# Per-node sums of a graph network: tile sums stored in DRAM and gathered again, or added in place into one turned tile in SBUF

## The chip, the cores and the metric

The kernel runs on one core of one Trainium2 chip. The time is the device time of one launch in microseconds; a kernel's time is the median of its runs. One more execution was recorded by the profiler; all rows below are of that one.

## What is computed

A graph of 12,500 nodes and 412,500 edges, sorted by their destination node, goes through two small networks. What matters here are the five places in which rows of edges are added up by destination.

```python
x = _layernorm(x + _L0_gnn_ref(x, edges, edge_weight, ...))    # two GCN convolutions: in each
    msg = xw[r] * norm[:, None]                                # one row of 16 (after moving W) for an edge
    out = segment_sum(msg, c, num_segments=num_nodes)
x = _layernorm(x + _L1_gnn_ref(x, edge_attr_8, src, dst, ...))
    n, e = _ln(_mlp(node_feat)), _ln(_mlp(edge_feat))          # encoders, width 64
    for s in range(2):
        ce = concatenate([e, n[senders], n[receivers]])
        e = e + _ln(_mlp(ce, ...)) * g + beta                  # 64 features for an edge
        agg = segment_sum(e, receivers, num_segments=num_nodes)
        n = n + _ln(_mlp(concatenate([n, agg]), ...))
    return _mlp(n)
```

## The kernel before

**Tiles and steps.** The edges are padded to 3232 tiles of 128; since they are sorted, a tile's destinations lie in a window of 128 nodes that begins at its first destination. One step of an edge loop takes G = 8 tiles; there are 403 steps (`NIST`). Nodes stand as 128 partitions times C = 98 (12544 places).

**The program** is a row of blocks with a barrier between them: tables, weights, edge loop g1, `conv1`, edge loop g2, `conv2`, node phase ne, edge loop s0, node phase n0, edge loop s1, node phase n1. g1 carries the first convolution's messages (16 columns) and the edge encoder (64): FS = 80 columns; g2 carries the second convolution's messages (16); s0 and s1 are the two edge blocks (64 columns, `expand`).

**One step.** `drive` (L573 is its loop of 8 steps an iteration, 50 iterations, with the steps before and behind written out) calls each engine's `step`; the engines meet by semaphores alone, and each runs its own instructions in order. A chunk of 8 tiles goes through stages a step apart (`L_BW` to `L_SUM`). POOL issues 8 indirect gathers of 128 rows for the senders (L720) into one of 8 buffers, and waits for the buffer: for the message product's mark `v_msg` in g1 and g2, for PE's mark `p_pre` in s0 and s1. SP loads their indices (L689) every fourth step, and in s0 and s1 the copies of destination numbers (L700) and four of the eight windows `Bw` of receivers' rows (L669); ACT loads the other four and `z` (L680). DVE makes the one-hot `P` (edge against place in the window, L608), in s0 and s1 the turned one-hot `Pt` for the receivers (L741), in g1 and g2 the message columns of `R` (L749), then the layer norm (L754, L756, Newton steps L140 to L149, `R` at L762) and in s0 the sum `rT` (L734). ACT does the squares, the activation `hT`, and copies.

**The sums.** PE multiplies for each of the 8 tiles P by R (L863: P as 128x128 weights, FS columns moving) into the PSUM tile `psw`: row w of a tile's product is the sum for the w-th node of its window. ACT copies psw to `sg` (L793), which frees psw (`a_seg`), and stores it (L808) to the tensor `seg_d` in DRAM. A node may have edges in several tiles, whose windows overlap only where one tile ends and the next begins. So behind each loop (`Sums`) POOL gathers each tile's last row (26 gathers, L931), PE turns them (L954), DVE multiplies and scans along the chain of tiles (L971, L974), PE turns the result back (L960), it is added to `seg_d` by DMA, and POOL gathers each node's row (98 gathers, L944) into `agg`. After g1 conv1 takes 16 of the 80 columns and POOL adds the other 64, with the norm's gain, to the second half of `NA`, which holds [nodes | sums] 128 wide; n0 and n1 add their sums to the same half, plus count times bias, and turn its 128 columns as the MLP's input in groups of four columns of nodes (8 stages).

## Time and profile before

| | us |
|---|---|
| median of 3 runs | 23702.86 (23700.19 to 23767.57) |
| the profiled execution | 23779.25 |
| its span, first to last instruction | 23777.4 |
| mean granted TensorE clock | 0.627 of 2.4 GHz |

| engine | busy us | share | instructions |
|---|---|---|---|
| TensorE (PE), matmul | 12398.6 | 52% | 61970 |
| VectorE (DVE) | 7767.6 | 33% | 22504 |
| ScalarE (ACT) | 2986.5 | 13% | 5247 |
| GpSimd (POOL) | 12971.1 | 55% | 13518 |

Shares over the span mix eleven blocks with different limits; the table of stretches below, with one row for a block, is to be read before them. "Idle before" in a row is time in which the engine stood still just before that instruction, and the name behind it is what ended that; "remote" is a semaphore of another engine that the profile can't place, "issue" is no wait that it shows.

### The profile page before, as it was taken

How to read it: one execution, taken by the hardware profiler on the slowest of the kernel's cores; microseconds unless marked ns; L12 is line 12 of the kernel's file. 1: busy time of each engine (PE TensorE's matmuls, PEld its weight loads, DVE VectorE, ACT ScalarE, POOL GpSimd, SP SyncE). 2: the span in 40 equal slices, each digit the busy share in tenths (PEclk: the TensorE clock that was granted, in tenths of full speed). 3: DMA queues.
4: the chain of work that ended last, by engine and by line, in shares of the span. 5: the costliest groups of instructions: out<-in, count | busy, mean ns of one | idle time of the engine just before them, and what ended most of it. 6: DMA issues, size and time to landing. Idle time of an engine off the chain costs nothing. (4 is left out here: it accounts for less than half of the span.)

```text
span 23777.4 us, 256036 instructions
## 1 busy us (share of the span) xinstructions
PE 12398.6 (52%) x61970; PEld 9600.5 (40%) x61970; DVE 7767.6 (33%) x22504; ACT 2986.5 (13%) x5247; POOL 12971.1 (55%) x13518
## 2 busy tenths in 40 slices
PE   0555565554232322325555656655556666666665
PEld 0444444443222222223444444444434444544454
DVE  2333333333111111112334434333333344343342
ACT  0222222221000000001111111111111111111111
POOL 2556565655666666662555555455435555555552
PEclk9566555565555555555667666666666666666675
DMA  1122222221000000001333333333323333333330
GB/s 50 52 54 56 54 55 55 55 55 47 12 11 11 11 11 11 11 11 22 99 102 107 107 102 104 103 105 104 103 60 94 100 98 99 99 99 98 99 101 14
DMA packets 2031268, 1570.78 MB, mean 66 GB/s; under 512 B 1340117, under 2 KB 1497177, under 8 KB 2029449
## 3 DMA queue, kind: packets, MB, share of 16 engines
q10 hardware_dynamic: 932082, 898.84, 11.7%
q0 software_dynamic: 446304, 295.04, 8.6%
q1 hardware_dynamic: 652511, 373.44, 5.7%
q14 instruction: 319, 2.61, 0.0%
q8 instruction: 52, 0.85, 0.0%
HBM read 961.50 MB, written 604.22 MB: 66 GB/s over the span
## 5 line engine op out<-in xcount | busy, mean ns | idle before, releaser
L720 POOL DMA_INDIRECT s_gt<-ta_d,s_ix x6448 | 6187.6, 960 | 5660.7 <-DMA s_ix<-in_src_s 2441.5
L863 PE MATMUL psw<-g_R,g_P 128*128 128x80 f32 (+1 forms) x12896 | 2673.2, 372 | 4261.8 <-ACT g_sg L793 3414.1
L863 PEld LDWEIGHTS psw<-g_R,g_P 128*128 128x128 f32 x12896 | 2568.8, 305 | 4795.9 <-issue 3827.8
L720 POOL DMA_INDIRECT g_gt<-xs_d,g_ix x3224 | 3048.8, 946 | 2077.7 <-DVE g_R L749 1106.8
L720 POOL DMA_INDIRECT g_gt<-ys_d,g_ix x3224 | 3049.7, 946 | 1798.9 <-issue 990.0
L608 DVE TENSOR_TENSOR g_P<-ps,dlT 128x1024 f32<-128x1024 f32 x806 | 985.3, 1222 | 5610.4 <-remote 4927.6
L863 PEld LDWEIGHTS psw<-s_R,s_P 128*128 128x128 f32 x12896 | 1908.9, 222 | 1705.1 <-issue 1702.8
L863 PE MATMUL psw<-s_R,s_P 128*128 128x64 f32 x12896 | 1877.4, 298 | 1057.3 <-issue 1020.0
L831 PE MATMUL ps<-e_w,s_hT 128*128 128x128 f32 x6448 | 1342.6, 375 | 1956.5 <-ACT s_hT L788 1679.1
L848 PE MATMUL ps<-s_Pt,s_Bw 128*64 128x128 f32 x12896 | 1535.7, 370 | 1009.8 <-issue 1008.2
L831 PEld LDWEIGHTS ps<-e_w,s_hT 128*128 128x128 f32 x6448 | 1181.8, 274 | 2084.2 <-ACT s_hT L788 1346.1
L848 PEld LDWEIGHTS ps<-s_Pt,s_Bw 128*64 128x64 f32 x12896 | 1118.1, 189 | 1358.4 <-issue 1356.4
L831 PE MATMUL ps<-e_w,g_hT 128*128 128x128 f32 x3224 | 768.4, 416 | 1266.4 <-issue 795.4
L734 DVE SCALAR_TENSOR_TENSOR s_rT<-ps,gct,s_z 128x512 f32<-128x512 f32 x403 | 302.1, 750 | 3179.4 <-DMA e_d<-s_rT 3081.6
L851 PE MATMUL ps<-s_z,zw 128*128 128x512 f32 x1612 | 1280.0, 881 | 84.3 <-issue 83.7
L831 PEld LDWEIGHTS ps<-e_w,g_hT 128*128 128x128 f32 x3224 | 700.7, 320 | 1325.3 <-issue 830.7
L793 ACT ACTIVATE g_sg<-psw 128x640 f32<-128x640 f32 (+1 forms) x806 | 395.7, 491 | 6599.3 <-remote 5304.3
L608 DVE TENSOR_TENSOR s_P<-psw,dlT 128x1024 f32<-128x1024 f32 x806 | 980.3, 1216 | 611.6 <-remote 529.4
L788 ACT ACTIVATE s_hT<-ps 128x512 f32<-128x512 f32 x806 | 480.4, 596 | 4303.1 <-remote 3728.9
L754 DVE TENSOR_REDUCE s_ss<-s_sq 128x8 f32<-128x512 f32 x806 | 547.1, 679 | 1371.9 <-issue 795.6
L741 DVE TENSOR_SCALAR s_Pt<-s_dl,iop 128x1024 f32<-128x1024 bf16 x806 | 612.8, 761 | 991.0 <-remote 806.1
L779 ACT ACTIVATE s_sq<-ps 128x512 f32<-128x512 f32 x806 | 481.4, 597 | 3553.5 <-issue 2016.2
(289 smaller groups left out, 12961.8 us busy)
## 6 DMA issues: line engine op xcount, KB each, us to landing
s_dl<-dl_d SPq DMA_DIRECT2D x404, 512.0 KB
seg_d<-s_sg ACTq DMA_DIRECT2D x806, 256.0 KB
seg_d<-g_sg ACTq DMA_DIRECT2D x403, 320.0 KB
z_d<-g_rT ACTq DMA_DIRECT2D x403, 256.0 KB
s_z<-z_d ACTq DMA_DIRECT2D x403, 256.0 KB, 3.0
s_Bw<-tb_d ACTq DMA_DIRECT2D x3224, 32.0 KB
s_Bw<-tb_d SPq DMA_DIRECT2D x3224, 32.0 KB
s_gt<-ta_d,s_ix POOLq DMA_INDIRECT x6448
```

What stands on the lines that cost most here:

```text
L608: return eng.tensor_tensor(P[:, :, :], bc(columns.rearrange("p (o e) -> p o e", o=1), [128, G, 128]), bc(dlT[:, bass.ds(j * G, G)].rearran ...
L720: eng.indirect_dma_start(out=gt[k][:, s, :], out_offset=None, in_=table[:, :], in_offset=bass.IndirectOffsetOnAxis(ap=ix[h][:, r * G + s:r ...
L734: eng.scalar_tensor_tensor(out=rT[k][:, :], in0=ps[5][:, :], scalar=gct[1][:, 0:1], in1=zt[kz][:, :], op0=ALU.mult, op1=ALU.add).then_inc( ...
L741: eng.tensor_scalar(Pt[t % 2][:, :], dl[h][:, t % 2 * G * 128:(t % 2 + 1) * G * 128], iop[:, 0:1], None, ALU.is_equal).then_inc(v_pt.sem, 1)
L754: eng.reduce_sum(ss[:, :], sq[k][:, :, :], axis=AX.X)
L779: eng.activation(sq[k][:, :, :].rearrange("p s f -> p (s f)"), ps[2 + k][:, :], ACT.Square).then_inc(a_sq.sem, 1)
L788: eng.activation(hT[k][:, :], ps[k][:, :], ACT.Silu).then_inc(a_h.sem, 1)
L793: eng.activation(sg[k][:, :].rearrange("p (t f) -> p t f", t=G), psw[:, 0:G * SP_].rearrange("p (t f) -> p t f", t=G)[:, :, 0:FS], ACT.Cop ...
L831: eng.matmul(ps[2 + k][:, 128 * q:128 * q + 128], hT[k][:, 128 * q:128 * q + 128], mlp[0][:, :], start=q == 0, stop=False, skip_group_chec ...
L848: eng.matmul(ps[k][half:half + 64, 128 * q:128 * q + 128], Bw[(b - L_PRE) % 4][:, t, :], Pt[k][:, 128 * t:128 * t + 128], start=False, sto ...
L851: eng.matmul(ps[k][:, :], (e_w0 if attr else zw)[:, :], zt[(b - L_PRE) % DZ][:, :], start=not expand, stop=True, skip_group_check=True).th ...
L863: last = eng.matmul(psw[:, SP_ * t:SP_ * t + FS], P[k][:, s, :], R[k][:, s, :], start=True, stop=True)
```

## The change

One SBUF tile `acc` of 128 partitions by 12544 + 128 columns holds the sums turned: column = node, row = feature. Rows 0 to 63 are the edge features, 64 to 79 the convolution's messages, row 80 the number of edges of a node. It is zeroed on POOL (at the end of the weights' block; rows 64 to 79 again in conv1) and kept over all loops.

PE's tile product is turned: R is the weights (80, 16 or 64 columns), P moves (128 columns), and the result is feature by place in the window, in `psw[LO:HI, 128 t]`. The 8 products come in two halves, each with its own mark `p_seg`. At the start of a step (stage `L_ACC` = 7) DVE loads four addresses for a half, waits for that half of the chunk before, and adds four times 128 columns of psw to `acc` at a column known only at run time, with a drain behind each since windows overlap; `v_acc` frees the half of psw. The norm's gain is the scalar of that addition (`accg`); g2 has none. Its bias, times the node's count in row 80, comes into the node MLP as a row of the weights `nb_wa`.

Gone are seg_d, sg, ACT's copy and store of it, the class `Sums` with its gathers, scans, transposes and stores, and the tables for them. conv1 and conv2 take their 16 rows from `acc` by 98 small matmuls (`by_node`) and add them from PSUM. The nodes' tile is 64 wide (`ND`); the node phases turn 64 columns and multiply `acc` directly by `nb_wa` (four matmuls a group); their POOL programs go.

`Pt` moves from DVE to ACT: `off` = Square(dl - p), then Relu(1 - off), two passes of 128x1024 behind `hT`; SP's load of dl and PE wait for its mark `a_pt`.

```diff
+        L_BW, L_Z, L_PT, L_PRE, L_LN, L_SEG, L_ACC, L_SUM, L_ST = 2, 2, 3, 4, 5, 6, 7, 7, 7
...
+        def half_done(eng, sem, j, off, h):
+
+            v = (j - off) * 2 + h + 1
+            if not isinstance(v, int) or v > 0:
+                eng.wait_ge(sem.sem, v + sem.base)
...
+            LO = 0 if mlp else 64
+            HI = LO + FS
...
-                            done(eng, v_pt, j, 3)
+                            done(eng, a_pt, j, 3)
...
+                        if stage(j, L_ACC):
+                            for h in range(2):
+                                _, at = nc.values_load_multi_w_load_instructions(
+                                    basei[32:33, bass.ds((j - L_ACC) * G + 4 * h, 4)], engines=[mybir.EngineType.DVE], min_val=0, max_val=N,
+                                    skip_runtime_bounds_check_because="a tile's first dst is a node's number")
+                                half_done(eng, p_seg, j, L_ACC, h)
+                                for t in range(4):
+                                    sums = acc[LO:HI, bass.ds(at[t], 128)]
+                                    new = psw[LO:HI, 512 * h + 128 * t:512 * h + 128 * t + 128]
+                                    if scale is None:
+                                        last = eng.tensor_tensor(sums, new, sums, ALU.add)
+                                    else:
+                                        last = eng.scalar_tensor_tensor(out=sums, in0=new, scalar=scale[LO:HI, 0:1], in1=sums,
+                                                                        op0=ALU.mult, op1=ALU.add)
+                                    if t < 3:
+                                        eng.drain()
+                                last.then_inc(v_acc.sem, 1)
+                                eng.drain()
...
-                        if stage(j, L_PT) and expand:
-                            t = b - L_PT
-                            h = (t // 2) % 2
-                            done(eng, p_pre, j, L_PT + 2)
-                            eng.wait_ge(s_dl[h].sem, (i * 2 + t // 4 + 1) * 16 + s_dl[h].base)
-                            eng.tensor_scalar(Pt[t % 2][:, :], dl[h][:, t % 2 * G * 128:(t % 2 + 1) * G * 128], iop[:, 0:1], None,
-                                              ALU.is_equal).then_inc(v_pt.sem, 1)
...
-                            done(eng, p_seg, j, L_LN + 2)
+                            half_done(eng, p_seg, j, L_LN + 2, 1)
...
-                        if stage(j, L_SEG):
+                        if stage(j, L_SEG) and attr:
                             k = (b - L_SEG) % 2
-                            done(eng, p_seg, j, L_SEG)
-                            landed(eng, s_so, 1, i, b, L_SEG + 2)
-                            eng.activation(sg[k][:, :].rearrange("p (t f) -> p t f", t=G),
-                                           psw[:, 0:G * SP_].rearrange("p (t f) -> p t f", t=G)[:, :, 0:FS],
-                                           ACT.Copy).then_inc(a_seg.sem, 1)
-                            if attr:
-                                done(eng, p_rt, j, L_SEG)
-                                landed(eng, s_ro, 1, i, b, L_SEG + 2)
-                                eng.activation(rT[k][:, :], ps[5][:, :], ACT.Copy, scale=gct[0][:, 0:1]).then_inc(a_rt.sem, 1)
+                            done(eng, p_rt, j, L_SEG)
+                            landed(eng, s_ro, 1, i, b, L_SEG + 2)
+                            eng.activation(rT[k][:, :], ps[5][:, :], ACT.Copy, scale=gct[0][:, 0:1]).then_inc(a_rt.sem, 1)
+                        if stage(j, L_PT) and expand:
+                            t = b - L_PT
+                            h = (t // 2) % 2
+                            done(eng, p_pre, j, L_PT + 2)
+                            eng.wait_ge(s_dl[h].sem, (i * 2 + t // 4 + 1) * 16 + s_dl[h].base)
+                            done(eng, a_pt, j, L_PT + 1)
+                            eng.activation(off[:, :], dl[h][:, t % 2 * G * 128:(t % 2 + 1) * G * 128], ACT.Square,
+                                           bias=niop[:, 0:1]).then_inc(a_off.sem, 1)
+                            done(eng, a_off, j, L_PT)
+                            eng.activation(Pt[t % 2][:, :], off[:, :], ACT.Relu, scale=-1.0, bias=one1[:, 0:1]).then_inc(a_pt.sem, 1)
...
-                        if stage(j, L_ST):
-                            k = (b - L_ST) % 2
-                            done(eng, a_seg, j, L_ST)
-                            settle(eng, s_m[0])
-                            eng.dma_start(seg_rows[:, bass.ds((j - L_ST) * (G * FS), G * FS)], sg[k][:, :]).then_inc(s_so[k].sem, 16)
...
-                            done(eng, a_seg, j, L_SEG + 1)
-                            for s in range(G):
-                                t = SLOT_TILE[s]
-                                last = eng.matmul(psw[:, SP_ * t:SP_ * t + FS], P[k][:, s, :], R[k][:, s, :],
-                                                  start=True, stop=True)
-                            last.then_inc(p_seg.sem, 1)
+                            for h in range(2):
+                                half_done(eng, v_acc, j, L_SEG + 1, h)
+                                for t in range(4 * h, 4 * h + 4):
+                                    s = TILE_SLOT[t]
+                                    last = eng.matmul(psw[LO:HI, 128 * t:128 * t + 128], R[k][:, s, :], P[k][:, s, :],
+                                                      start=True, stop=True)
+                                last.then_inc(p_seg.sem, 1)
...
-        class Sums:
...
+        def by_node(eng, sem):
+
+            for n, (q, m) in enumerate(BANKS):
+                for k in range(m):
+                    last = eng.matmul(ps[n][:, 16 * k:16 * k + 16], accn[64:80, q + k, :], ident[64:80, 64:80], start=True, stop=True)
+                last.then_inc(sem.sem, 1)
...
-                sums_of("ns80", seg80_d, 80, agg, lambda eng: eng.tensor_tensor(NA[:, :, 64:128], cb, bb, ALU.mult))
...
-                    eng.tensor_tensor(agg[:, :, 0:64], agg[:, :, 0:64], gb, ALU.mult).then_inc(g_agg.sem, 1)
-                    eng.wait_ge(*g_agg(1))
-                    eng.tensor_tensor(NA[:, :, 64:128], NA[:, :, 64:128], agg[:, :, 0:64], ALU.add)
+                    eng.wait_ge(*p_agg(len(BANKS)))
+                    eng.memset(acc[64:80, :], 0.0)
...
+                    by_node(eng, p_agg)
...
-                    eng.tensor_tensor(tx[:, :, :], tx[:, :, :], agg[:, :, 64:80], ALU.add)
+                    for n, (q, m) in enumerate(BANKS):
+                        eng.wait_ge(*p_agg(n + 1))
+                        eng.tensor_tensor(tx[:, q:q + m, :], tx[:, q:q + m, :], bank(n), ALU.add)
...
-                sums_of("ns16", seg16_d, 16, agg)
...
-                            eng.matmul(ps[1][0:64, 0:W], w0[:, :], xT[k][:, 0:W], start=True, stop=True).then_inc(n_h.sem, 1)
+                            last = eng.matmul(ps[1][0:64, 0:W], w0[:, :], xT[k][:, 0:W], start=True, stop=wa is None, skip_group_check=True)
+                            for i in range(m if wa is not None else 0):
+                                last = eng.matmul(ps[1][0:64, 128 * i:128 * i + 128], wa[:, :], accn[0:81, g + i, :],
+                                                  start=False, stop=i == m - 1, skip_group_check=True)
+                            last.then_inc(n_h.sem, 1)
```

How the instructions of DVE stand in the loop of g2, each step ending with the message product `g_R`. Before (`g_gt` are the gathered rows, `ew` the weights, `dlT` the destinations):

```order
L608 ISA [waits e_pseg]
L608 TENSOR_TENSOR g_P<-ps,dlT 128x1024
L749 REGISTER_ALU [waits e_g5]
L749 TENSOR_TENSOR g_R<-g_gt,ew 128x128
L573 REGISTER_ALU
```

And after, one half of the adds and what follows the second:

```order
L740 TENSOR_TENSOR g_R<-g_gt,ew 128x128
L712 ISA
L712 TENSOR_LOAD basei
L599 ISA
L720 ISA [waits e_pseg]
L720 TENSOR_TENSOR acc<-psw,acc 16x128
L720 ISA
...
L580 ISA [waits e_pseg]
L580 TENSOR_TENSOR g_P<-ps,dlT 128x1024
L571 ISA
L740 REGISTER_ALU [waits e_g6]
```

Before, P was the first thing behind the wait for PE's tile sums; now eight adds and two address loads stand between g_R and the next P.

DVE in the loop of s0, from the norm's `s_R` to the one-hot. Before:

```order
L762 TENSOR_TENSOR s_R<-ps,s_yy 128x512 [waits e_prt]
L599 ISA [waits e_prt]
L734 SCALAR_TENSOR_TENSOR s_rT<-ps,gct,s_z 128x512 [waits e_ro0]
L591 REGISTER_ALU
L741 TENSOR_SCALAR s_Pt<-s_dl,iop 128x1024 [waits e_dl1,e_ppre]
L591 REGISTER_ALU
L608 ISA [waits e_pseg]
L608 TENSOR_TENSOR s_P<-psw,dlT 128x1024
```

After:

```order
L753 TENSOR_TENSOR s_R<-ps,s_yy 128x512 [waits e_prt]
L712 ISA
L712 TENSOR_LOAD basei
L599 ISA
L722 ISA [waits e_pseg]
L722 SCALAR_TENSOR_TENSOR acc<-psw,accg,acc 64x128
L722 ISA
...
L571 ISA [waits e_prt]
L732 SCALAR_TENSOR_TENSOR s_rT<-ps,gct,s_z 128x512 [waits e_ro0]
L580 ISA [waits e_pseg]
L580 TENSOR_TENSOR s_P<-ps,dlT 128x1024
```

The adds stand ahead of s_rT and its wait; s_Pt has left the engine.

## Rows read from the trace of the kernel before

**Rows 1.** The table of stretches, one for a block: us, busy (instructions), clock, DMA
```profile
521.50:5653.00 5131.50, 2986.84 (x12493) 2313.26 (x12493) 1955.94 (x6449) 1265.07 (x2016) 3048.77 (x3224) 0.60 0.21 54
...
5956.00:10792.00 4836.00, 1438.09 (x6448) 1405.04 (x6448) 573.63 (x807) 112.13 (x404) 3049.67 (x3224) 0.50 0.10 11
...
11021.50:11267.00 245.50, 240.49 (x902) 153.06 (x902) 91.19 (x400) 70.27 (x126) 0.00 (x0) 0.58 0.12 27
11267.00:17382.00 6115.00, 3588.39 (x20553) 2644.74 (x20553) 2418.94 (x6852) 693.37 (x1211) 3095.39 (x3224) 0.69 0.38 104
17382.00:17763.50 381.50, 186.53 (x1006) 132.19 (x1006) 149.11 (x531) 70.43 (x127) 148.69 (x128) 0.70 0.18 35
17763.50:23193.00 5429.50, 3516.04 (x18941) 2638.15 (x18941) 2149.78 (x6449) 691.86 (x1211) 3092.19 (x3224) 0.68 0.37 98
23193.00:23777.40 584.40, 349.08 (x1227) 242.41 (x1227) 167.19 (x573) 72.52 (x126) 148.98 (x128) 0.55 0.07 13
```

The busy columns are PE, PEld, DVE, ACT, POOL.

**Rows 2.** POOL's waits in g1, g2 and s1: us in total, times, longest
```profile
POOL g_gt L720 <- DVE g_R L749: 1106.8, 243, 15.1
...
POOL g_gt L720 <- DVE g_R L749: 749.0, 97, 15.7
...
POOL s_gt L720 <- DMA s_ix<-in_src_s: 857.3, 97, 171.8
```

**Rows 3.** Timeline of g1: start, us, engine, line, operation, [idle before]
```profile
3020.91 1.23 DVE L608 TENSOR_TENSOR g_P<-ps,dlT 128x1024 f32<-128x1024 f32 x1 [4.15 <-remote]
...
3022.06 3.70 PE L863 MATMUL psw<-g_R,g_P 128*128 128x80 f32 x16
...
3023.12 0.95 POOL L720 DMA_INDIRECT g_gt<-xs_d,g_ix  x1 [5.61 <-DVE g_R L749]
```

**Rows 4.** Timeline of g2
```profile
8024.00 1.22 DVE L608 TENSOR_TENSOR g_P<-ps,dlT 128x1024 f32<-128x1024 f32 x1 [26.71 <-remote]
...
8026.20 0.95 POOL L720 DMA_INDIRECT g_gt<-ys_d,g_ix  x1 [7.88 <-DVE g_R L749]
...
8028.05 1.22 DVE L608 TENSOR_TENSOR g_P<-ps,dlT 128x1024 f32<-128x1024 f32 x1 [2.63 <-PE psw L863]
```

**Rows 5.** Between the loops: a group of gathers, then timeline rows of n0, conv1, conv2
```profile
L944 POOL DMA_INDIRECT n_agg<-seg_d,gidx x196 | 186.1, 949 | 73.3 <-issue 59.2 <-DMA seg_d<-n_ns_L 14.1
...
17472.18 1.08 POOL L944 DMA_INDIRECT n_agg<-seg_d,gidx  x1 [7.09 <-DMA seg_d<-n_ns_L]
...
5870.97 15.04 DVE L1089 TENSOR_TENSOR tx<-xf,dis 128x1568 f32<-128x1568 f32 x1 [145.04 <-PEq L32]
...
11000.51 1.79 DVE L1136 TENSOR_TENSOR agg<-agg,ys 128x1568 f32<-128x1568 f32 x1 [140.67 <-PEq L32]
```

**Rows 6.** DVE's groups by line and form: busy us, mean ns, idle before
```profile
L741 DVE TENSOR_SCALAR s_Pt<-s_dl,iop 128x1024 f32<-128x1024 bf16 x806 | 612.8, 761 | 991.0 <-remote 806.1 <-issue 176.6 <-DMA s_dl<-dl_d 8.3
...
L145 DVE TENSOR_TENSOR s_tt<-s_yy 128x8 f32<-128x8 f32 x2418 | 415.5, 172 | 180.2 <-issue 1.2
...
L1315 DVE TENSOR_TENSOR n_rr<-ps,n_yy 128x256 f32<-128x256 f32 x48 | 20.4, 425 | 3.9 <-issue 0.4
...
L968 DVE COPY ns_LT<-ps 80x128 f32<-80x128 f32 x26 | 6.4, 287 | 36.5 <-PE ps L954 35.1
```

**Rows 7.** Line 665 in s1, duration in ns: smallest, median, largest
```profile
L665 ACTq TENSOR_LOAD <-basei x329: 311/315/338, 18608.5 to 22997.1; - x165
```

**Rows 8.** DVE's waits in s0, 12000 to 17000 us
```profile
DVE s_rT L734 <- DMA e_d<-s_rT: 2612.7, 276, 29.9
```

**Rows 9.** PE's groups in s0 and s1, from the page: busy us, mean ns
```profile
L863 PE MATMUL psw<-s_R,s_P 128*128 128x64 f32 x12896 | 1877.4, 298 | 1057.3 <-issue 1020.0
...
L848 PE MATMUL ps<-s_Pt,s_Bw 128*64 128x128 f32 x12896 | 1535.7, 370 | 1009.8 <-issue 1008.2
```

**Rows 10.** Line 573, DVE at the loop's end in s1: ns, first and last start
```profile
L573 DVEq COMPARE_BRANCH  x41: 62/63/63, 18686.3 to 22965.0; - x41
...
L573 DVEq FUSED_REGOPS  x41: 62/63/63, 18690.3 to 22968.5; - x41
```

361 lines of the change are left out of this document (112 added, 249 removed).

## The prediction

> **What bounds the kernel now.** I read the table of stretches first, then who waits for whom on POOL, then two cycles of the timeline, then the durations. By the stretches [rows 1] four edge loops of 403 steps take 21,512 of the 23,777 us: 12.73, 12.00, 15.17 and 13.47 us a step for g1, g2, s0 and s1; what lies between and behind them takes 303.0 us for conv1 (from g1's end to g2's start), 229.5 for conv2, 245.5 for ne, 381.5 for n0 and 584.4 for n1. In every loop POOL's busy time is 3,049 to 3,095 us: 8 gathers a step at 0.95 us, 1.25 us from start to start. So 10.0 us a step is POOL issuing, and 2.0 to 5.2 us is POOL stopped. VectorE (DVE) is busy 4.9, 1.4, 6.0 and 5.3 us a step: never the bound now.
>
> Why does POOL stop? In g1 and g2 it waits for DVE's `g_R` (L749), 1,107 and 749 us, in 243 and 97 waits; in s1 the long waits are for the index load, 857 us [rows 2]. The timeline shows what is behind the first two. In g1 [rows 3] POOL had stopped at 3017.51 (3023.12 less 5.61); DVE starts the one-hot P only at 3020.91, after 4.15 us idle, the product g_R follows it, and POOL starts 2.2 us behind P's start: 3.4 + 2.2 = 5.6 us. Two steps go into each such cycle: 20 + 5.6 us. In g2 [rows 4] DVE had been idle for 26.71 us, P starts at 8024.00, and POOL's stop was 7.88 us; the next step then follows 4.05 us behind (8028.05). Four steps go into such a cycle: 40 + 7.9 us = 12.0 each, which is the loop's mean. PE's signals that DVE waits for come late while POOL issues without a break, and soon after it stops. I take that as a given of the trace; its cause I can't see.
>
> **The change, part by part.** The sum is made against the profiled execution: 23,779 us, 76 us (0.3%) above the median of 23,703; the forecast is brought to the median at the end. 0.3%, some 71 us, is what a measurement can tell.
>
> *Gone, and sure.* Between the loops the sums' machinery vanishes. In n0 the 90 us of last rows, transposes, scan and stores ahead of the first gather of node sums (17382 to 17472.18) go, and the first node group no longer waits for 24 gathers, each 1.32 us ((186.1 + 73.3)/196), 32 us [rows 5]; the rest of its 291 us behind the first gather is about the pace of the groups themselves, for which ne needs 245.5 us [rows 1]. The four new matmuls of a group cost some 12 us in all: -110. n1 likewise, -122. conv1: 217 us of sums (5653 to 5870) go, and a DVE operation that takes 15.04 us beside POOL's long additions takes 1.79 at conv2 without them [rows 5]; there are two such, -27 together. In come 98 matmuls at up to 0.37 us (the means of [rows 9]), 36 us, and the adds of four banks, about 8: +44. Sum: -200. conv2: 208 us of sums (10792 to 11000.5 [rows 5]) against +45: -163. In the tables three stores and a scan go: -15, from nearly nothing to 30. **Between the loops: -610 us**, between -500 and -680.
>
> A rule of the Trainium skill fits these rows (SBUF — State Buffer, "Who interferes with whom"): a DVE operation with two SBUF inputs and a GpSimd one exclude each other for a whole instruction. The trace agrees at conv1 with 15.04 against 1.79 us. By the same rule the new adds, which read one operand from PSUM, would not be held by POOL; the sum takes nothing for it.
>
> *Added on DVE, every step:* eight adds of 128 elements a partition from PSUM into `acc`, a drain behind each, and two loads of four addresses. An add lies between the copy of 128 from PSUM, 0.287 us, and the 256-element operation from PSUM, 0.425 [rows 6]; the middle is 0.345, with 0.07 for the drain (what lies between DVE's small operations that drain, 180.2 us in 2418 [rows 6]) and 0.065 for the address's register work, my guess between nothing and the 0.13 that would double it: 0.48, eight times 3.85. An address load is 0.31 us on ScalarE (ACT) [rows 7]; with its registers 0.4, twice 0.8. In all **4.65 us a step** (4.2 in g2, whose adds have no scalar), bounds 3.6 and 5.6. DVE loses the receivers' one-hot in s0 and s1, 0.76 us [rows 6]; ACT gets two passes of 128x1024 for it (each at most about DVE's 1.22 for as many elements [rows 4]) and loses the tile sums' copy and store; it is busy 11 to 25% now and I count nothing. DVE's step becomes 10.4, 5.8, 10.8 and 10.1 us with its gaps: as long as POOL's 10.0, where it was half.
>
> *Where the adds lie.* They stand ahead of P and g_R, behind the same late signal. In **g1**, first half's signal now comes when PE is halfway through its 16 matmuls (3.7 us [rows 3], so 1.85 early); the second half's adds and loads, and the rest of the first, come on top: 4.65 - 1.85 = 2.8 us longer for POOL's stop, in a cycle of two steps +1.4 a step. Some of the 243 waits are shorter than that cycle's, so I take +1.15: **+463 us**, bounds 0 (adds done before the signal matters) and +2.3 a step, +937. In **g2** 4.2 - 1.8 = 2.4 us in four steps, +0.6: **+242**; bounds 0 and, if a cycle holds only three steps because a step in the quick part now takes 5.8 instead of 4.05 us, (30 + 9.7)/3 = 13.2, +490. In **s0** POOL doesn't wait for DVE, and DVE itself waits before L734 for 2,613 us in 330 steps (5,000 us at 15.17), 7.9 each [rows 8]: the adds stand right ahead of that wait and fill it: **0**, bounds -0.43 and +0.6 a step. The lower bound is PE's: tile sums cost 1877.4/12896 = 0.146 us each now, and the matmul with the shape they get (64 columns of weights, 128 moving), L848, 0.119 [rows 9]; 16 of them are 0.43 us a step, which I count at nothing, since POOL and not PE stands at 15.17. The stores gone are 256 KB a step of DMA traffic; nothing waited for them. In **s1** PE's products wait for R, which comes 4 us later in a step with 3 us of room: +0.15, **+60**, bounds -0.43 and +0.6.
>
> Loops: 463 + 242 + 0 + 60 = **+765 us**. With -610: **+155**; 23,779 + 155 = 23,934 for the profiled execution, 23,858 against the median: **23,860 us**, 0.7% slower.
>
> **The rivals.** *The adds cost nothing* (faster). DVE idles 26.7 us before the late signal in g2 and 4 to 8 in g1; if half signals come early enough for the adds to run in that idle time, the loops stay as they are and only the 610 us count: 23,093; with PE's 0.43 us in both s loops (-345) 22,750. For it: DVE is 28 to 40% busy, and POOL's 10 us are untouched. Against it: in [rows 3, 4] P and g_R start the moment the signal comes, so anything put between moves POOL's start.
>
> *The adds in full* (slower). The half signal comes no earlier, because both halves are late together; g1 +937 and g2 at three steps a cycle +490; 1,427 - 610 = +817, 24,520 against the median. This decides once the four loops lose more than 610/1612 = 0.38 us a step on average; the forecast has 0.47.
>
> *DVE's program gets too long.* In s1 DVE passes its loop's end in 4.0 us (18686.3 to 18690.3) [rows 10] where the branch takes 0.06; such a pass in each of 50 iterations of g1 and s0 as well is up to 400 us: on top of the forecast 24,260. For it: the bodies grow from 155 and 173 rows to 332, drains not counted. Against it: DVE has room in s0, and POOL runs on meanwhile.
>
> **Chances.** The forecast 0.42, adds hidden 0.25, in full 0.20, long program 0.13. The forecast's own terms spread by some 200 us either way, so it lends 0.09 to faster and 0.12 to the same. Faster by over 0.3%: 0.34; within: 0.12; slower: 0.54. The forecast's own range is 23,650 to 24,100; to leave out no more than 2 in 10 the range goes from 23,050, the hidden adds, to 24,600, the adds in full.
>
> **What would show it.** In the profile after: g1 near 13.9 and g2 near 12.6 us a step, s0 near 15.2, s1 near 13.6; conv1 near 100 us, conv2 near 65, n0 near 270, n1 near 460. POOL's stop in g2 near 10 us every fourth step, with eight adds between DVE's late start and g_R; one add at 0.35 us, start to start 0.48. In s0 the wait of L734 shrunk by about 4 us a step. It is wrong if g1 or g2 keeps its step, if POOL comes to wait for DVE every step, or if s0 and s1 move by more than 0.6 us a step either way: then PE's signals, not POOL, set those loops.

## The result: 4.9% slower, and the profile after

The changed kernel takes 24,885 us (median of 4 runs, 24,864 to 24,901); the kernel before, run beside it, 23,724 (23,700 to 23,768). The ratio is 1.0487, with a 95% interval of 1.0467 to 1.0506. The forecast was 23,860 us with a range up to 24,600: slower was right, the size was not, and the time lies outside the range.

The profiled execution spans 24,890 us, 1,113 more than before's 23,777. The table of stretches of the changed kernel, cut as in [rows 1]: after the stretch come its us, then the busy time (instructions) of PE, PE's weight loads, DVE, ACT and POOL, the granted clock, the DMA share and GB/s.

```profile
521.00:6471.00 5950.00, 3139.02 (x12482) 2477.58 (x12483) 3063.01 (x9665) 963.45 (x1612) 3050.56 (x3224) 0.58 0.10 25
6471.00:6581.50 110.50, 99.48 (x358) 81.87 (x358) 21.27 (x64) 10.07 (x27) 10.65 (x1) 0.50 0.04 14
6581.50:11592.00 5010.50, 1478.58 (x6451) 813.20 (x6451) 1508.85 (x4031) 0.00 (x0) 3049.60 (x3224) 0.52 0.06 6
11592.00:11895.50 303.50, 279.28 (x1097) 194.75 (x1096) 111.05 (x425) 70.28 (x126) 0.00 (x0) 0.58 0.10 22
11895.50:18077.00 6181.50, 3694.96 (x20533) 2582.71 (x20533) 3225.64 (x9645) 1357.17 (x1613) 3049.35 (x3224) 0.71 0.31 86
18077.00:18381.50 304.50, 289.55 (x1118) 199.87 (x1118) 110.88 (x453) 70.40 (x126) 0.00 (x0) 0.61 0.10 24
18381.50:24465.00 6083.50, 3430.21 (x18941) 2367.42 (x18941) 2965.73 (x9270) 1358.67 (x1613) 3049.11 (x3224) 0.70 0.27 70
24465.00:24890.30 425.30, 377.21 (x1319) 258.12 (x1319) 117.70 (x469) 72.53 (x126) 0.00 (x0) 0.56 0.01 2
```

In order they are g1, conv1, g2, conv2 with ne, s0, n0, s1, n1. Against [rows 1] the blocks between the loops give what was promised: conv1 303.0 to 110.5, conv2 with ne 475.0 to 303.5, n0 381.5 to 304.5, n1 584.4 to 425.3; together -600 us (-610 forecast). The four loops lose 1,713 us (765 forecast): g1 12.73 to 14.76 us a step, g2 12.00 to 12.43, s0 15.17 to 15.34, s1 13.47 to 15.09. So two terms of the forecast are wrong: **g1, +2.03 a step for +1.15, and s1, +1.62 for +0.15**.

**g1.** POOL's waits in g1 of the changed kernel (us in total, times, longest); the first row answers to 1,107 us in 243 waits in [rows 2]:

```profile
POOL g_gt L700 <- DVE g_R L740: 1813.9, 286, 18.3
POOL g_gt L700 <- issue: 1001.5, 2937, 10.6
POOL g_gt L700 <- DMA g_ix<-in_src_s: 47.3, 1, 47.3
```

POOL still waits for DVE, longer. What does DVE wait for? First g1 of before, the three largest rows:

```profile
DVE g_P L608 <- remote: 1386.7, 198, 36.9
DVE g_ss L754 <- issue: 1108.0, 191, 34.2
DVE g_ss L754 <- ACT g_sq L779: 246.7, 203, 4.9
```

and g1 of the changed kernel:

```profile
DVE acc L722 <- issue: 1571.0, 2953, 6.0
DVE g_mq L142 <- issue: 180.7, 269, 1.5
DVE g_P L580 <- issue: 153.5, 392, 1.8
DVE g_yy L144 <- issue: 136.4, 211, 1.3
DVE g_tt L140 <- issue: 132.2, 202, 1.3
DVE acc L722 <- remote: 77.3, 12, 22.9
```

Before, DVE stood still twice in every second step: some 200 times for P, 7 us each, and some 200 times for `g_ss`, 6 us each (the profile calls these "issue", so the word alone is no proof that an engine waited for nothing). Now the waits put down to other engines and to DMA come to some 170 us in the whole loop, and DVE's idle time lies in thousands of short gaps ("issue": nothing that the profile shows released it). A step of DVE holds 7.60 us busy (3063.01/403) and 7.16 idle. Its largest group in g1, the adds (busy, mean ns, then idle before them):

```profile
L722 DVE SCALAR_TENSOR_TENSOR acc<-psw,accg,acc 80x128 f32 x3216 | 1116.6, 347 | 1723.3 <-issue 1571.0 <-remote 77.3 <-PE psw L853 69.9
```

From start to start an add takes (1116.6 + 1723.3)/3216 = 0.88 us, loads and waits included, where the forecast had 0.48, or 0.58 with the address loads (4.65/8). The timeline of g1 (start, us, engine, line, [idle before]) shows both kinds:

```profile
3019.29 0.35 DVE L722 SCALAR_TENSOR_TENSOR acc<-psw,accg,acc 80x128 f32 x1 [2.88 <-issue]
3021.42 0.35 DVE L722 SCALAR_TENSOR_TENSOR acc<-psw,accg,acc 80x128 f32 x1 [1.79 <-issue]
3022.85 0.35 DVE L722 SCALAR_TENSOR_TENSOR acc<-psw,accg,acc 80x128 f32 x1 [1.08 <-issue]
3023.35 0.35 DVE L722 SCALAR_TENSOR_TENSOR acc<-psw,accg,acc 80x128 f32 x1 [0.15 <-issue]
3023.76 2.00 PE L853 MATMUL psw<-g_P,g_R 128*80 128x128 f32 x8 [8.73 <-DVE acc L722]
3024.44 0.35 DVE L722 SCALAR_TENSOR_TENSOR acc<-psw,accg,acc 80x128 f32 x1 [0.73 <-issue]
3024.94 0.35 DVE L722 SCALAR_TENSOR_TENSOR acc<-psw,accg,acc 80x128 f32 x1 [0.15 <-issue]
```

An undisturbed add stands 0.50 us behind the last; but three of the first half's four came 1 to 3 us late, beside POOL's last gathers and right behind them, and PE waited 8.73 us for them, because the adds free `psw`.

The stops of POOL, counted in both traces as gaps between two gathers, show what became of the forecast's cycle. Before, POOL stopped 195 times for over 5 us, 5.6 on average. After, it stops 180 times for over 5 us, 9.1 on average (the forecast: 5.6 + 2.8 = 8.4), and 191 more times for 1 to 5 us, 1.5 on average, where before it did so twice. The longer stops are 1.4 us of the lost 2.0 a step, the new short ones 0.7. In g2 the waits for g_R read

```profile
POOL g_gt L700 <- DVE g_R L740: 928.7, 191, 16.5
```

against 749.0 in [rows 2]. The stops over 5 us didn't grow (7.7 us before, 7.5 after), they came more often: 118 for 97.

**s1.** POOL's waits in s1, after; its long ones are still for the index load and for released buffers:

```profile
POOL s_gt L700 <- DMA s_ix<-in_src_s: 1656.8, 92, 396.6
POOL s_gt L700 <- issue: 941.4, 2978, 3.9
POOL s_gt L700 <- remote: 435.9, 118, 12.2
POOL s_gt L700 <- PE ps L840: 299.5, 36, 14.4
```

and before, beside the 857.3 for the index load in [rows 2]:

```profile
POOL s_gt L720 <- remote: 629.9, 196, 12.0
POOL s_gt L720 <- PE ps L851: 21.8, 5, 8.7
```

One wait of each index row lies ahead of the loop's first gather, while the nodes are computed: 171.8 us before, 396.6 after, when POOL has no work there any more. Without it the index load is waited for 575 us longer (1260.2 for 685.5), PE's products, which release POOL's buffers, 278 us longer, and "remote" 194 us shorter: together 659 us, the lost 1.6 us a step. SP issues the index load, behind the load of `dl` in one queue, and that waits for `Pt`, which ACT now makes; PE's products wait for `Pt` too.

### The profile page after: what moved, and what is told of

Read it like the earlier page. It is cut to its first block and busy times, and to the rows that moved or that the text cites. A ratio compares the mean times of both kernels' runs of the same rounds, so it can differ in the third digit from the quotient of the medians.

```text
span 24890.3 us, 296537 instructions
## 1 busy us (share of the span) xinstructions
PE 12793.7 (51%) x62338; PEld 8979.1 (36%) x62338; DVE 11285.5 (45%) x34276; ACT 3904.1 (16%) x5246; POOL 12323.2 (50%) x13007
## 3 DMA queue, kind: packets, MB, share of 16 engines
q14 instruction: 1189, 9.74, 0.1%
## 5 line engine op out<-in xcount | busy, mean ns | idle before, releaser
L853 PE MATMUL psw<-g_P,g_R 128*80 128x128 f32 (+1 forms) x12896 | 3069.8, 418 | 6303.0 <-DVE acc L720 2421.8
L722 DVE SCALAR_TENSOR_TENSOR acc<-psw,accg,acc 64x128 f32 (+1 forms) x9672 | 3333.1, 345 | 5298.9 <-issue 4569.5
L853 PEld LDWEIGHTS psw<-g_P,g_R 128*80 128x80 f32 (+1 forms) x12896 | 2104.2, 192 | 7533.4 <-DVE acc L720 2651.0
L853 PE MATMUL psw<-s_P,s_R 128*64 128x128 f32 x12896 | 2245.9, 330 | 2550.7 <-DVE acc L722 1383.7
L853 PEld LDWEIGHTS psw<-s_P,s_R 128*64 128x64 f32 x12896 | 1776.9, 167 | 3558.1 <-DVE acc L722 1793.0
L720 DVE TENSOR_TENSOR acc<-psw,acc 16x128 f32 x3224 | 933.8, 290 | 3242.3 <-issue 2265.2
L580 DVE TENSOR_TENSOR s_P<-ps,dlT 128x1024 f32<-128x1024 f32 x806 | 984.1, 1221 | 225.3 <-issue 221.0
L784 ACT ACTIVATE g_rT<-ps,gct 128x512 f32<-128x512 f32 x403 | 277.0, 687 | 4302.9 <-remote 3036.2
L794 ACT ACTIVATE s_Pt<-s_off,one 128x1024 f32<-128x1024 bf16 x806 | 925.6, 1148 | 26.4
L791 ACT ACTIVATE s_off<-s_dl,niop 128x1024 bf16<-128x1024 bf16 x806 | 918.6, 1140 | 10.6 <-DMA s_dl<-dl_d 10.6
```

The lines of the kernel that those rows point to most:

```text
L580: return eng.tensor_tensor(P[:, :, :], bc(columns.rearrange("p (o e) -> p o e", o=1), [128, G, 128]), bc(dlT[:, bass.ds(j * G, G)].rearran ...
L720: last = eng.tensor_tensor(sums, new, sums, ALU.add)
L722: last = eng.scalar_tensor_tensor(out=sums, in0=new, scalar=scale[LO:HI, 0:1], in1=sums, op0=ALU.mult, op1=ALU.add)
L791: eng.activation(off[:, :], dl[h][:, t % 2 * G * 128:(t % 2 + 1) * G * 128], ACT.Square, bias=niop[:, 0:1]).then_inc(a_off.sem, 1)
L794: eng.activation(Pt[t % 2][:, :], off[:, :], ACT.Relu, scale=-1.0, bias=one1[:, 0:1]).then_inc(a_pt.sem, 1)
L853: last = eng.matmul(psw[LO:HI, 128 * t:128 * t + 128], R[k][:, s, :], P[k][:, s, :], start=True, stop=True)
```

## Experiments

The hypotheses, by letters that the texts on record use too: **R**, the address loads and register instructions of the adds are slow while POOL issues; **N**, the number and time of DVE's instructions (its step is as long as POOL's, so all of it counts, wherever it stands); **W**, the place of the adds between the late signal and g_R; **P**, `Pt` by two ACT operations, 2.3 us in place of DVE's 0.76; **F**, DVE's program fetched anew in every iteration.

The runs were made on five chips, each with the kernel before beside them. The chips differ: the kernel before took 23,509 us on chip A1 and 23,739 on A3, near the 23,724 of the result, but 18,410, 18,419 and 18,413 on B2, B4 and B5. Each chip was used once, so whether the chip makes the difference or its state at that time isn't shown. On B the loops of *ptact* and *best* run at POOL's own 10.0 us a step, or up to 0.2 above. Only ratios within a chip count. The table gives them with their intervals, and us a step from POOL's 89th gather of a loop to its last (the first steps left out, so most values are some 0.1 under those of the stretches). The row "before" is of the profile shown ahead; A1's own is 0.9% faster by its median, some 0.1 us a step, so that a difference of 0.1 there means nothing.

```
kernel           chip  ratio to before          g1     g2     s0     s1
before           A     1                        12.62  11.94  15.07  13.36
changed          A     1.0487 (1.0467-1.0506)   14.64  12.38  15.21  14.95
fixed            A1    1.0317 (1.0298-1.0336)   13.60  12.18  15.20  14.66
noadd            A1    1.0010 (1.0001-1.0020)   12.50  11.72  15.27  14.51
pad              A1    1.0400 (1.0381-1.0420)   13.06  12.10  15.20  14.34
merged           A1    1.0172 (1.0153-1.0191)   13.34  11.79  15.24  14.54
after_again      A3    1.0470 (1.0433-1.0507)   14.57  12.33  15.21  14.95
pt_back          A3    1.0256 (1.0220-1.0291)   14.43  12.36  14.60  14.34
pt_act_again     A3    1.0406 (1.0366-1.0445)   12.63  11.95  15.44  15.23
best_again       A3    0.9517 (0.9485-0.9549)   12.53  11.76  13.92  13.36
ptact            B2    1.0009 (0.9999-1.0018)   10.02  10.03  10.16   9.99
busy             B2    1.0858 (1.0840-1.0876)   11.03  10.92  11.11  11.31
late             B2    1.0472 (1.0455-1.0490)   10.63  10.02  11.95  10.48
best             B2    0.9763 (0.9747-0.9780)   10.02  10.01  10.15  10.17
late_again       B4    1.0466 (1.0447-1.0486)   10.64  10.02  11.91  10.51
late_pt          B4    1.0492 (1.0472-1.0513)   10.62  10.02  11.57  10.94
best_pause       B4    1.2860 (1.2839-1.2882)   13.45  13.45  13.64  13.91
late_third       B5    1.0457 (1.0438-1.0475)   10.62  10.03  11.86  10.49
after_third      B5    1.0421 (1.0404-1.0438)   10.81  10.02  11.33  10.73
best_pause1      B5    1.1739 (1.1719-1.1758)   12.24  12.14  12.25  12.79
```

### Chip A1: the adds taken apart

*fixed*: the eight adds go to fixed columns, so the address loads and register work are gone (the sums land in the wrong places).

```diff
-                                _, at = nc.values_load_multi_w_load_instructions(
-                                    basei[32:33, bass.ds((j - L_ACC) * G + 4 * h, 4)], engines=[mybir.EngineType.DVE], min_val=0, max_val=N,
...
-                                    sums = acc[LO:HI, bass.ds(at[t], 128)]
+                                    sums = acc[LO:HI, 128 * t:128 * t + 128]
```

> The changed kernel, but each add goes to a fixed column of acc (0, 128, 256 or 384) instead of the tile's own: no address load and no address register work on VectorE; the eight adds, their drains and waits stay. (The node sums are therefore not placed.) In the changed kernel g1 takes 14.76, g2 12.43, s0 15.34 and s1 15.09 us a step, and in each loop some 2,000 register instructions of VectorE last over 0.6 us, 1,550 to 1,780 us in all, about 4 us a step. Theory R (register work and address loads are what is slow while GpSimd issues): they are gone, g1 falls to about 12.8 to 13.2, s1 to about 13.6; in all about 23,400. Theory F (VectorE's long loop body is fetched anew in each iteration and starved): the body still has some 390 instructions in g1 and s0, other instructions take over the slow starts, g1 stays above 14, in all 24,400 or more. Theory W (the adds' own 3.8 us behind the late signal): g1 near 14.3, in all about 24,500.

g1 gets back 1.04 of its 2.02 us a step, g2 0.20, s1 0.29. So about half of g1's loss is the address work (R), less than R had forecast (g1 at 12.8 to 13.2). Of the 2,000 long ones that the text above counts in g1, some 770 are register instructions and address loads; the rest are drains. The adds in g1 of *fixed*, and what DVE waits for there:

```profile
L719 DVE SCALAR_TENSOR_TENSOR acc<-psw,accg,acc 80x128 f32<-80x128 f32 x3148 | 1088.7, 346 | 986.7 <-issue 403.2 <-remote 365.3 <-PE psw L850 62.9
```

```profile
DVE g_ss L742 <- ACT g_sq L767: 912.5, 87, 31.8
```

The "issue" gaps ahead of the adds fall from 1,571 to 403 us, and DVE waits for others again. The add itself (346 ns) costs the same.

*noadd*: no adds at all; the waits stay, and `psw` is freed at once (the sums are left out).

> The changed kernel without the adds: VectorE waits for each half of the tile sums and frees it at once, nothing is added (the node sums are left out). All theories expect what lies between the loops to stay as in the changed kernel, some 600 us less than before. If the adds are the whole loss, g1 returns to 12.7, g2 to 12.0, s1 to 13.5 and s0 to 15.2 us a step or less: about 23,100 in all. If moving the receivers' one-hot to ScalarE is what costs s1, s1 stays near 15.1: about 23,700.

g1 and g2 are 0.12 and 0.22 us a step under before: all that these two loops lose hangs on the adds and their address work. But s1 stands at 14.51, 1.15 above before, **without an add in the kernel**: most of s1's loss has another cause. POOL's waits in s1 of *noadd*:

```profile
POOL s_gt L700 <- DMA s_ix<-in_src_s: 1209.2, 61, 386.6
POOL s_gt L700 <- PE ps L826: 548.8, 43, 14.3
```

Without its first wait the index load stands at 823 us, 137 above before; PE's products stand 527 above.

*pad*: the kernel before with 28 drains at the end of DVE's step, as many more instructions as the change adds.

```diff
+                        for _ in range(28):
+                            eng.drain()
```

> The kernel before with 28 drains more at the end of VectorE's step: its loop bodies grow from about 259, 44, 283 and 265 recorded instructions to about 480, 270, 500 and 490, as long as in the changed kernel, with about 1 to 2 us of engine time a step, no register work, no address load and no wait. Theory F: the instruction packets of its queue rise from about 10 in a loop (253 in s1) to about 250 to 300 in each; VectorE starts late while GpSimd issues, and g1 and s1 rise by 0.5 to 1.5 us a step: 24,100 to 24,900. Theories R and W: nothing is behind the signal and VectorE has 5 us of room, so within 0.3% of 23,724.

4% from drains alone: g1 +0.44, g2 +0.16, s0 +0.13, s1 +0.98. DVE had no free room in s1, although its busy share there was 5.3 of 13.5 us [rows 1]. In g1 the drains, which stand behind g_R, cost a fifth of what the adds do. F had forecast this size (24,100 to 24,900; it came to 24,470), R and W nothing; a price on the number of DVE's instructions (N) gives it as well.

*merged*: one add a step. PE adds up the eight tiles in one bank over a window that begins at the step's first destination (1024 sorted edges touch far fewer than 128 nodes here, which this version relies on).

```diff
-                                for t in range(4):
-                                    sums = acc[LO:HI, bass.ds(at[t], 128)]
...
+                            sums = acc[LO:HI, bass.ds(at[0], 128)]
...
+                            for s in range(G):
+                                last = eng.matmul(psw[LO:HI, o:o + 128], R[k][:, s, :], P[k][:, s, :],
+                                                  start=s == 0, stop=s == G - 1)
```

> The changed kernel with one add a step instead of eight: TensorE sums the eight tiles of a step into one window in PSUM that begins at the step's first destination (the 1024 edges of a step span at most 34 nodes in these inputs, which the kernel relies on), in one of two banks; VectorE adds those 128 columns to acc: one address load, one add. Its loop body shrinks to about 300 instructions. All theories expect the loss in the loops to go: g1 12.7 to 13.0, g2 12.0, s0 15.0 and s1 13.5 or less, 23,100 in all. Theory F with a threshold between 283 and 300 instructions would leave a part in g1 and s0.

g1 +0.72, g2 -0.15, s1 +1.18, which is *noadd*'s. At 1.7% above before it missed what all had forecast (23,100). As to F, the queue of the instructions (packets, MB, share) in the changed kernel's page:

```profile
q14 instruction: 1189, 9.74, 0.1%
```

Before has 319 packets, *fixed* 799, *noadd* 70, *merged* 312. *noadd* has the fewest, and s1's loss; *merged* has before's number, and a loss in g1. The fetches rise from *noadd* to the changed kernel with the length of DVE's program, but they don't order the losses, and on chip B5 the changed kernel has the same 1189 with half the gap per add (below). The Trainium skill (Runtime: NRT & Kernel Launch, "Instruction fetch mechanics") says why they rise: a branch out of the window that an engine keeps has to fetch again; the trace agrees in the count alone. No run prices a fetch, so that they are part of the gaps in the changed kernel's g1 isn't excluded.

### Chip A3: the one-hot on ScalarE

Four kernels on one A chip. *pt_back* is the changed kernel with `Pt` by one DVE operation again; *pt_act_again* the kernel before with `Pt` by ACT and nothing else.

```diff
+                            eng.activation(off[:, :], dl[h][:, t % 2 * G * 128:(t % 2 + 1) * G * 128], ACT.Square,
+                                           bias=niop[:, 0:1]).then_inc(a_off.sem, 1)
...
+                            eng.activation(Pt[t % 2][:, :], off[:, :], ACT.Relu, scale=-1.0, bias=one1[:, 0:1]).then_inc(a_pt.sem, 1)
...
-                            eng.tensor_scalar(Pt[t % 2][:, :], dl[h][:, t % 2 * G * 128:(t % 2 + 1) * G * 128], iop[:, 0:1], None,
-                                              ALU.is_equal).then_inc(v_pt.sem, 1)
```

> The changed kernel with one part undone: the receivers' one-hot Pt is made by one VectorE operation again, in the place it had before, instead of two passes of ScalarE. Theory P (the two passes of ScalarE end later, and with them the free buffer that the next dl and index loads wait for, so that s1 pays): s1 falls by 0.8 to 1.2 us a step (320 to 480 us) against the changed kernel, s0 stays within 0.3. Theory N (VectorE's and ScalarE's number of instructions sets it, wherever they stand): VectorE gets longer by 0.76 us a step, and s1 rises or stays within 0.3 of the changed kernel. g1 and g2 don't use Pt: unchanged. On a chip where POOL stops for nobody (18,400 us): s0 and s1 within 0.2 us a step either way.

> The kernel before with that one part alone: Pt by two passes of ScalarE, the gathered tile sums and everything else as before. It was within 0.1% on a chip with POOL bound in all loops, which can't tell. Theory P: where s1 stops for the index load, s1 rises by 0.8 to 1.2 us a step, 1.3 to 2.1% in all, with no add in the kernel. Theory N: unchanged or faster by VectorE's 0.76 us, within 0.3%.

The part that I had "counted at nothing" makes the kernel before **4.1% slower by itself**: s1 +1.87, s0 +0.37 us a step, more than P gave it. Where it shows: SP's wait for `Pt`, and POOL's for the index load, in s1 of before:

```profile
SPq L603 <- DVE s_Pt L741: 1176.8, 114, 60.1
```

(with POOL's 857 us of [rows 2]), and in s1 of *pt_act_again*:

```profile
SPq L607 <- ACT s_Pt L807: 2068.7, 140, 39.1
POOL s_gt L725 <- DMA s_ix<-in_src_s: 1717.8, 99, 171.0
```

POOL waits 860 us longer for the index load, 2.1 us a step. The timeline of *pt_act_again* shows why ACT is late with it: in its order `Pt` stands behind the copy of the tile sums, which had waited 13.56 us; SP issues the `dl` load (its queue rows start with SPq) 0.6 us after `Pt` ends. The changed kernel has no such copy in s1; there `Pt` stands right behind `hT`, which waits 1,948 us in all for "remote", in 212 times.

```profile
20104.12 0.60 ACT L791 ACTIVATE s_sg<-psw 128x512 f32<-128x512 f32 x1 [13.56 <-remote]
20104.61 1.14 ACT L804 ACTIVATE s_off<-s_dl,niop 128x1024 bf16<-128x1024 bf16 x1
20105.79 1.15 ACT L807 ACTIVATE s_Pt<-s_off,one 128x1024 f32<-128x1024 bf16 x1
20107.53 0.72 SPq L705 DMA_DIRECT2D s_dl<-dl_d  x1
```

*pt_back* returns 0.61 us a step in s0 and in s1 (P had 0.8 to 1.2 for s1 and at most 0.3 for s0), and leaves s1 0.98 above before: the share of the adds and the turned sums. In s1 the one-hot costs 1.87 in the kernel before and 1.15 in *noadd* (net of what that kernel saves elsewhere), the adds 0.98, both together 1.6: they overlap. Two ways carry the delay to POOL: the queue with the `dl` and index loads, and the product that needs `Pt` and releases POOL's buffer. In *pt_act_again* nearly all of the rise is in the wait for the index load, in *noadd* most of it in the wait for PE's products. The two weren't separated by a run (*dl4*, with four `dl` buffers, had no room in SBUF and gave no result). And SP's wait by itself is no price: in *pt_back* it is 2,589 us in s1, more than in *pt_act_again*, with less of a loss.

*after_again* is the changed kernel once more.

> The changed kernel once more, unedited, as the measure for the other kernels on this chip. Where the kernel before takes near 23,500 us (POOL stopping 2 to 5 us a step behind late signals), 1.047 to 1.050 of it; where it takes near 18,400 us (POOL bound, 10.0 us a step in every loop), the adds should matter only where DVE's step passes 10 us: g1 about 10.6 to 13, and 1.04 to 1.06 in all.

1.0470 after 1.0487, so the two A chips agree, and the numbers of A1 and A3 may be set beside each other with the care said above.

*best_again* has one add a step, behind P and g_R, and `Pt` on DVE. (*best*, below, is the same kernel.)

> Merged sums (one add a step instead of eight), the add behind P and g_R, and Pt on VectorE. It was 0.976 where POOL is bound. If late signals stop POOL on this chip: between the loops -600 us, g1 and g2 within 0.3 us a step of the kernel before since nothing new stands ahead of g_R, s0 and s1 within 0.3: 0.970 to 0.985. If the late regime alone prices the number of VectorE's instructions: g1 +0.7 us a step still, 0.985 to 1.0.

22,599 us against 23,739: **4.8% faster than before and 9% faster than the changed kernel**, more than the 0.970 to 0.985 expected. Besides the 600 us it gains 1.15 us a step in s0. The tile sums' copies and stores are gone there, PE's products are turned and summed, and `Pt` is in its old place; which of these gives the gain wasn't separated. In the changed kernel its two costs had covered it.

Its g1 stands at 12.53, where *merged*, the same single add ahead of P, has 13.34. In g1 the two kernels differ by that place alone (`Pt` isn't used there). They are from different chips, on which the changed kernel's g1 agrees within 0.1 (14.64 and 14.57): so where signals come late the place of even one add is worth some 0.8 us a step, and W is part of g1's loss. No pair of runs on one A chip shows it.

### Chips B2, B4 and B5: POOL doesn't stop

*ptact* is *pt_act_again*'s kernel.

> The kernel before with one part of the change alone: the receivers' one-hot is made by ScalarE in two passes behind hT, and VectorE no longer makes it. Without any adds (run noadd) s1 still took 14.51 us a step against 13.36 before, s0 15.27 against 15.07. Theory P (the one-hot on ScalarE ends 2.8 us behind TensorE's late signal instead of 0.75, SyncE's load of the next destinations waits for it, and the index load queued behind that load comes a step later): s1 rises to 14.3 to 14.6, s0 to 15.2 to 15.3, in all about 23,950. Rival: the turned tile sums, in halves, are what slows TensorE in s1: then this kernel stays within 0.3% of the kernel before.

Nothing there: s0 and s1 run at POOL's pace. The same edit costs 4.1% on one chip and 0.1% on another.

*busy*, the kernel before with three DVE operations of 128x1400 a step, was to separate time from number.

> The kernel before with three long VectorE operations (128x1400, about 1 us each, one drain behind each) at the place where run pad had 28 drains: the same 3 us of engine time that the 28 drains take at their quickest, in 6 instructions instead of 28. Run pad cost 4.0%; in it a step's 28 drains took 6.6 us at the median, 3.2 at the least. Theory N (the number of instructions that VectorE has to start while GpSimd issues counts, some 0.7 us for each, not their work): within 0.5% of before. Theory W (busy time in VectorE's chain counts wherever it lies): 2% to 4% slower as pad.

g2 rises too, by 0.9 us a step against *ptact*, although DVE has room there. POOL waits for nobody; its gathers themselves get longer, in *busy* and then in *ptact*:

```profile
L721 POOL DMA_INDIRECT g_gt<-ys_d,g_ix x3224 | 3416.9, 1060 | 1042.1 <-issue 982.2
L725 POOL DMA_INDIRECT g_gt<-ys_d,g_ix x3224 | 3057.3, 948 | 1042.3 <-issue 982.5
```

8 times 0.112 us is the 0.9. The gathers beside the three operations take 1.24 and 1.63 us (7003.75 and 7005.29), the others 0.94. So these operations delay POOL's own work, and the run, which lies above both forecasts, tells nothing on the question.

*late*: the changed kernel with the eight adds moved behind P and g_R. It ran three times (*late*, *late_again*, *late_third*), each time on a B chip (1.0472, 1.0466, 1.0457), so what the place of the eight adds is worth on an A chip wasn't measured.

> The changed kernel with the eight adds moved behind the one-hot P and the message product g_R, ahead of the layer norm, in each step. In g1 the adds no longer stand between TensorE's late signal and g_R. Theory W (their place): g1 falls from 14.64 to 13.0 us a step, g2 from 12.38 to 12.0, s loops unchanged: about 24,000 against 24,885 for the changed kernel. Theory N (VectorE's step with its slow starts is 14 us long and sets g1): g1 stays above 14, in all above 24,500.

*after_third* is the changed kernel beside it.

> The changed kernel beside it. Near 23,700 us of before: 1.047 to 1.050 again. Near 18,400 us of before: theory W, the place costs there too, since g_R comes 3 us later in each step and VectorE's step is longer than GpSimd's 10.0 in either case: g1 11 to 13 us a step and 1.07 to 1.12 in all. Theory N: g1 as in late, 10.6 us, and 1.04 to 1.055.

On the B chip the late place gains nothing in all: 1.0457 late, 1.0421 early (0.2 us a step less in g1 and s1, 0.5 more in s0). What costs in g1 is the length of DVE's step. In the timeline of g1 of *after_third* the first add of three steps in a row (start, us), and then the group of the adds:

```profile
3001.62 0.35 DVE L722 SCALAR_TENSOR_TENSOR acc<-psw,accg,acc 80x128 f32 x1
...
3012.36 0.35 DVE L722 SCALAR_TENSOR_TENSOR acc<-psw,accg,acc 80x128 f32 x1
...
3022.75 0.35 DVE L722 SCALAR_TENSOR_TENSOR acc<-psw,accg,acc 80x128 f32 x1
```

```profile
L722 DVE SCALAR_TENSOR_TENSOR acc<-psw,accg,acc 80x128 f32 x3152 | 1094.2, 347 | 886.4 <-issue 878.0 <-PE psw L853 0.6
```

10.7 and 10.4 us from step to step, and g1 at 10.81. Nearly all of DVE's idle time there is "issue", and POOL waits for its g_R 301 us, 0.75 a step:

```profile
POOL g_gt L700 <- DVE g_R L740: 301.1, 183, 4.4
```

DVE is the bound, and POOL's 10.0 us wait for it. An add takes (1094.2 + 886.4)/3152 = 0.63 us there, against 0.88 on the A chip, with the same 347 ns of work. The gap before it is 0.28 us on B and 0.54 on A.

*late_pt* adds `Pt` on DVE to *late*.

> Eight adds behind P and g_R, and Pt by VectorE: against best (one add, the same place, the same Pt) it differs by the number of adds alone, against late by Pt alone. Theory W and P together explain all: 0.955 to 0.975, s0 and s1 within 0.3 us a step of 13.9 and 13.4, g1 near 12.5. Theory N: the seven more adds, 3.3 to 4 us of VectorE a step, cost 0.5 us a step or more in g1, s0 and s1 each, and it ends above 0.985.

s0 falls by 0.3 against *late*, s1 rises by 0.4: where DVE is the bound, 0.76 us more on DVE costs, and the relief of ACT pays little. Against *best* (same place, same `Pt`, one add) it costs 0.6 us a step more in g1, 1.4 in s0 and 0.8 in s1. *best* also sums in PSUM, in two banks by turns, so that PE waits less for the adds. In g1 it is DVE's longer program all the same, since DVE waits for nobody there (895 of its 916 us idle are "issue"); in s0 and s1 the two weren't separated.

> The changed kernel with one add a step (as run merged: TensorE sums a step's eight tiles into one window), this add moved behind P and g_R, and the receivers' one-hot back on VectorE. From merged (g1 13.34, g2 11.79, s0 15.24, s1 14.54): if theory P holds s1 falls to 13.4 and s0 to 15.0; by theory W g1 falls to 12.5, as in noadd. All together 200 + 80 + 460 + 330 us under merged's 23,920: about 22,900, 2.5% faster than before.

*best_pause* and *best_pause1* are *best* with three wasted GpSimd memsets a step, or one, to see whether signals come late because POOL issues without a break.

> Best with three memsets of 128x512 by GpSimd ahead of each step's eight gathers, which are pure waste: some 1.5 us a step in which it issues no DMA. Where POOL is bound it must cost what it takes: 1.5 us a step, 1.03 against best. Theory C (signals of the other engines come late because GpSimd issues gathers without a break): the pause ends the late signals, POOL's stops vanish, and the loops fall to 11.5 to 12 us a step, below best. Theory D (the stops have another cause, a chain of work a step long): each loop stays as best, within 0.2, the pause hidden in the stops, or rises by up to 1.5.

> Best with one wasted memset of 128x512 by GpSimd and a drain ahead of each step's gathers; three of them with their drains cost 3.4 us a step where POOL is bound. Where POOL is bound: 1.1 to 1.7 us a step, 1.06 to 1.09 against best. Where late signals stop POOL: theory C (signals late because GpSimd issues without a break) all four loops at 11.2 to 11.9 us a step, s0's 13.9 and s1's 13.4 too; theory D (another cause) the loops at best's 12.5, 11.8, 13.9 and 13.4 or up to 1.2 above.

Both fell on B chips, where nothing is late; they cost 3.4 and 2.2 us a step in g1, 3.7 and 2.6 in s1. **Why signals are late on A chips stays open.**

## Why the prediction was wrong

**Between the loops: right.** -600 for -610. n0 kept 304.5 us for the 270 forecast, conv1 110 for 100; n1 is 425 for 460.

**An add's price: a term mis-sized.** I had 0.345 + 0.07 + 0.065 = 0.48 from start to start. The work was right (0.347) and so was the undisturbed add (0.50). But eight of them with their address loads take 7.1 us on this chip, not 4.65: the idle time ahead of each is 0.54 us on average, waits of 0.05 included. The 0.07 came from operations in the quiet part of DVE's step [rows 6], the register work was a guess, and I had no row of DVE's drains and registers beside busy gathers. *fixed* shows that the address work makes 1.0 us of g1's 2.0.

**DVE's step: the number was there, and not used.** The sum said that DVE's step becomes 10.4 us, "as long as POOL's 10.0", and then priced only the delay of g_R. On B chips the step is 10.4 and 10.7, and g1 takes 10.81: the sentence is literally right there. On the A chip a step is 14.8, nearly without waits for others. The model "POOL's stop grows by what stands before g_R" (+1.15) wasn't idle there: the long stops of every second step grew from 5.6 to 9.1 us, for the forecast's 8.4, which is 1.4 a step. What it lacked is the other 0.7: POOL now stops for DVE in nearly every step (371 stops over 1 us in 403 steps), because DVE has no room left. That is the sign of being wrong that the prediction named itself. How the 2.0 divide between the place of the adds and the length of DVE's step was not measured on an A chip. The rival "adds in full" had the same model with another size; its 24,520 came nearer, with longer stops (10.2 us) in every second step and none in between; they were 9.1, with short ones in between.

**g2: near by size, not by mechanism.** +0.43 a step for +0.6. DVE has room there (1508.85/403 = 3.7 us busy). But the stop was to grow to 10 us in every fourth step; it stayed at 7.5 and came more often.

**s0: zero came out by luck.** +0.17. The adds did fill the wait of L734, as forecast: of its 3,082 us, 271 are left. But under the zero lie a gain of 1.15 us a step (*best_again*; I had allowed at most 0.43) and the costs of the adds and of `Pt` that eat it (0.6 for `Pt`, *pt_back*).

**s1: the step that failed is "I count nothing".** Two ACT passes of 1.14 and 1.15 us (at most 1.22 each was the bound, so their size was right) in place of 0.76 on DVE were counted at nothing because ACT is busy 11 to 25%. But ACT's operations run in order, behind ones that wait for late signals (13.56 us in the timeline above), and SP's `dl` load with the index load behind it, and PE's product, wait for `Pt`. [rows 2] named the index load as s1's wait (685 of the 857 us lie in the loop): the edit was put on the path that sets the loop. The prediction priced it by a busy share, and had no rival for it. Alone it costs 1.15 to 1.87 us a step, and the changed kernel gets 0.61 back without it; the adds make the rest of the 1.62.

**The rivals.** Adds hidden: no; *noadd* shows what that would be, and even it is at 1.001, because s1 and s0 take nearly all that the blocks give. The long program: the fetches came; their share stays undecided, and their number explains neither s1 nor the order of the losses.

## What to carry to other kernels

When an edit brings an engine's own program, gaps included, to within a few per cent of the step, expect that engine to be the new bound: price the whole step, not only the delay at one signal. An engine's busy share doesn't tell whether an operation is free on it; ask what stands ahead of it in its order, and who waits for it, DMA queues and the loads behind them included. And take a sum of many small products on PE, in PSUM, before one engine adds it: one add a step behind the message product, with the one-hot back on VectorE, turned +4.7% into -4.8%.

## What the chip showed beyond that

The same kernel takes 23.5 to 23.7 ms on some chips and 18.4 on others: POOL's gathers take 0.95 us on both, but the gap before an add of DVE is 0.54 us on the first and 0.28 on the second. The traces show one thing more. These are the register instructions that set an add's address, in the changed kernel on an A and on a B chip (ns: smallest, median, largest):

```profile
L722 DVEq FUSED_REGOPS  x9672: 1/46/1421, 555.4 to 24464.7; - x198
L722 DVEq FUSED_REGOPS  x9672: 46/46/53, 541.5 to 18740.4; - x198
```

On A chips a register instruction that mostly takes 0.05 us takes 0.7 now and then, on the queues of DVE, ACT and SP: 3,011 of DVE's 23,823 last over 0.6 us in the first run. In the ten runs on B chips not one does. Within g1 DVE's register instructions and address loads take 1.1 us a step more on A than on B. So it is DVE's own stream that is stretched there; why, and whether PE's late signals have the same cause, stays open. An edit's worth goes with it: `Pt` on ACT 4.1% or 0.1%, *best* 4.8% or 2.4%. 28 drains that do nothing cost 4% where DVE was busy for 12 to 40% of a loop. One GpSimd memset of 128x512 with its drain, 0.54 us of work, costs 2.2 us a step between gathers:

```profile
2007.43 0.94 POOL L705 DMA_INDIRECT g_gt<-xs_d,g_ix  x1 [0.30 <-issue]
2008.37 0.54 POOL L702 MEMSET g_rest<- 128x512 f32 x1
2010.80 0.95 POOL L705 DMA_INDIRECT g_gt<-xs_d,g_ix  x1 [1.89 <-issue]
```
